# Four key tiles in one chunk for the steepest heads, weighted sums dealt in runs of 32, and an earlier turned K

## What is computed

```python
x = L0_attn_x                                    # [4, 2048, 256]
xn = _layernorm(x, axis=-1)
# attention
slopes = 2.0 ** (8.0 * arange(0, -H, -1) / H)    # H = 16: 1, 0.71, 0.5, ... 2**-7.5
scores = einsum('bhqd,bhkd->bhqk', q, k) / sqrt(16)
bias = -slopes[:, None, None] * abs(pos[None, :] - pos[:, None])
probs = softmax(scores + bias[None], axis=-1)
out = einsum('bhqk,bhkd->bhqd', probs, v)
s = out.transpose(0, 2, 1, 3).reshape(B, S, D) @ W_out.T + b_out
# experts: top 2 of 8 in one of two groups, weights normalised, plus a shared expert
y = einsum('tei,eih->teh', silu(x @ w_gate) * (x @ w_up), w_down)
g = silu(einsum('teh,te->th', y, comb) + shared)
return x + s * g
```

## Time and profile before

| | |
|---|---|
| Median of three runs (lowest, highest) | 1667.21 us (1664.34, 1673.85) |
| The profiled execution | 1676.03 us, of which the instructions span 1674.1 us |
| Busy over the span | PE 1524.8 us, ACT 1318.0 us, DVE 1010.6 us, PEld 680.6 us, POOL 496.4 us |
| Mean granted clock of TensorE | 0.976 |

### The profile page before, as it was taken

The page is one execution under the profiler, slowest core; times in us unless marked ns, Lnnn a source line. Parts: engine busy times, 40 slices in busy tenths (PEclk is TensorE's granted clock), DMA queues, the critical chain, the costliest instruction groups (busy, mean ns, idle before and its releaser), DMA issues. The chain is left out here.

```text
span 1674.1 us, 39958 instructions
## 1 busy us (share of the span) xinstructions
PE 1524.8 (91%) x15328; PEld 680.6 (41%) x15328; DVE 1010.6 (60%) x2738; ACT 1318.0 (79%) x1694; POOL 496.4 (30%) x477
## 2 busy tenths in 40 slices
PE   5898997899989999998999899989999899988996
PEld 3554564223334443343444333434443333322464
DVE  7787765988854454545445444454455444577776
ACT  5788776888888887887888788878888788788721
POOL 1222331000023343343343343434333333222053
PEclk9999998999999999999999999999999999999999
DMA  6858776233345455454444455544545554577795
GB/s 202 274 193 253 259 228 183 68 112 90 90 143 132 131 138 141 138 137 128 137 134 134 126 139 137 140 132 134 131 134 143 135 134 134 132 203 221 244 313 173
DMA packets 201089, 265.58 MB, mean 159 GB/s; under 512 B 90960, under 2 KB 158592, under 8 KB 200640
## 3 DMA queue, kind: packets, MB, share of 16 engines
q1 hardware_dynamic: 168256, 171.72, 36.8%
q0 software_dynamic: 24192, 82.86, 16.1%
q10 hardware_dynamic: 8448, 8.39, 1.4%
HBM read 180.56 MB, written 90.46 MB: 162 GB/s over the span
## 5 line engine op out<-in xcount | busy, mean ns | idle before, releaser
L1502 ACT ACTIVATE probs_att<-SC_att 128x1024 f32<-128x1024 f32 (+10 forms) x1306 | 1075.2, 911 | 181.5 <-PE SC_att L1385 160.4
L1411 PE MATMUL O_att<-probs_att,V_att 128*32 128x512 f32 (+7 forms) x8144 | 642.5, 412 | 50.3 <-DVE probs_att L1527 28.4
L1527 DVE TENSOR_TENSOR probs_att<-probs_att,decay 128x128 f32<-128x128 f32 x1024 | 264.3, 286 | 272.6 <-ACT probs_att L1502 245.9
L1411 PEld LDWEIGHTS O_att<-probs_att,V_att 128*32 128x32 f32 x8144 | 178.4, 111 | 208.7 <-issue 129.4
L1385 PE MATMUL SC_att<-Q,K_turned_att 64*128 64x512 f16 (+7 forms) x1244 | 221.6, 310 | 13.9 <-issue 5.6
L1334 POOL DMA_INDIRECT ys<-ys_att,back_of_att x144 | 144.7, 1005 | 252.9 <-ACT probs_att L1502 226.8
L1328 POOL DMA_INDIRECT x<-xn,row_of_att x144 | 142.8, 992 | 243.2 <-ACT probs_att L1502 226.3
L1385 PE MATMUL SC_att<-Q,K 64*128 64x512 f16 (+9 forms) x1154 | 201.2, 301 | 7.6 <-DVE K_turned_att L1514 7.0
L1385 PEld LDWEIGHTS SC_att<-Q,K_turned_att 64*128 64x128 f16 x1244 | 67.2, 94 | 265.2 <-ACT probs_att L1502 156.7
L1322 POOL DMA_INDIRECT x<-w_rows,owner x72 | 71.9, 999 | 333.6 <-DVE row_of_att L1576 217.3
L699 POOL TENSOR_TENSOR inverse<-qk_tok,inverse 128x512 f16<-128x512 f32 x64 | 75.6, 1189 | 171.4 <-ACT inverse L731 164.3
(11 more groups left out here) (212 smaller groups left out, 1672.4 us busy)
## 6 DMA issues: line engine op xcount, KB each, us to landing
K<-k_stack SPq DMA_DIRECT2D x86, 256.0 KB
Q<-q_stack SPq DMA_DIRECT2D x86, 256.0 KB
x<-ys POOLq DMA_DIRECT2D x32, 512.0 KB, 4.8
x<-in_x SPq DMA_DIRECT2D x24, 512.0 KB, 6.7
k_stack<-inverse SPq DMA_DIRECT2D x96, 128.0 KB
q_stack<-inverse SPq DMA_DIRECT2D x96, 128.0 KB
inverse<-k_stack SPq DMA_DIRECT2D x42, 256.0 KB
inverse<-q_stack SPq DMA_DIRECT2D x42, 256.0 KB
```

The costliest lines, as they stand in the source:

```text
L1411: mm = pe.matmul(O[VW * g:VW * (g + 1), col:col + width * len(mine)], V[par][:, k, :], spans[:, j0:j0 + BPB * (len(mine) - 1) + 1:BPB, :], ...
L1502: nc.scalar.activation(probs[home][:, side + chunk.base:side + chunk.base + chunk.width], SC[:, c % SLOTS, start:start + chunk.width], ACT ...
L1527: v.tensor_tensor(diag, diag, decay[:, head_of(chunk.head), :], ALU.mult).then_inc(faded, 1)
```

## The change

The change has five parts, all in the second stage.

1. A step takes four key tiles where two neighbouring tiles together have at most 512 queries and the next two as well (`steps_of`, `plan`). The first two tiles go to the left PSUM bank and the other two to the right one. This touches heads 0 to 2 alone: a steep head has 4 chunks of 960 or 1024 columns in place of 8 of 448 or 512 (in the first batch 4, 6 and 6 chunks in place of 8, 8 and 10). In all 1260 chunks and 794 steps are left. The columns stay the same.
2. Heads 3 to 10 are dealt to the strips in runs of 32 queries, heads 0 to 2 and 11 in runs of 64 as before (`DEALT`, `block_of`). The number of matmuls is the same, but the strips hold different counts. With 896 queries, for instance, the strips had four, four, three and three runs of 64, and have seven runs of 32 each. `store_head` follows: its pieces are 32 numbers long.
3. `fade` takes all the diagonals of a chunk in one instruction with a stride, where they lie at equal distances.
4. `turn_k` for the next head stands behind the first chunk of a head with fewer than 8 chunks. `stage_v` stays at the middle chunk.
5. `ROUTE_FROM` goes from 8 to 4 and `FF_EACH` from 11300 to 11200. The first tile of the experts is turned at column 210,240 in place of 204,160, and the last at column 1,003,776 in place of 1,005,184.

```diff
@@ -47,10 +47,10 @@
 WGU = 2 * DC * I
 WROW = WGU + D
 GROUP = 4
-ROUTE_FROM, SIDE_FROM, NORMS_AT = 8, 8, 5
+ROUTE_FROM, SIDE_FROM, NORMS_AT = 4, 8, 5
 PREFIX_TURNS, LIST_TURN, LISTED_AFTER, TILES_AFTER = (31, 36), 61, 136, 16
 FF_APART = (("turn", 2), ("gate", 3), ("down", 4))
-FF_EACH = 11300
+FF_EACH = 11200
 FF_PARTS = {"turn": ("turn", 0), "take": ("turn", 1), "gate": ("gate", 0), "up": ("gate", 0), "tanh": ("gate", 3), "hid": ("gate", 4),
             "down": ("down", 0), "y": ("down", 1)}
 MIX_FROM, MIX_TO = 364, 397
@@ -78,6 +78,7 @@
 FAR = (64, 192, 256, 256, 256, 320, 448, 576, 896, 1216, 1600, 1792)
 LIMITED = len(NEAR)
 LEFT_OUT = 2.0 ** -25
+DEALT = {h: 32 if 3 <= h < 11 else HALF for h in range(LIMITED)}
 ORDER = tuple(x for h in range(H // 2) for x in (h, H - 1 - h))
 STORED = 16 * (BPB + 1)
 
@@ -133,15 +134,17 @@
 
     if head_of(n) >= LIMITED:
         return [(kt,) for kt in range(KT)]
-    small = [window(n, kt)[1] - window(n, kt)[0] <= TB for kt in range(KT)]
+    size = [window(n, kt)[1] - window(n, kt)[0] for kt in range(KT)]
+    fits = lambda kt, count: kt + 2 * count <= KT and max(sum(size[kt:kt + count]), sum(size[kt + count:kt + 2 * count])) <= TB
     steps, kt = [], 0
     while kt < KT:
-        size = 2 if all(small[kt:kt + 2]) and len(small[kt:kt + 2]) == 2 else 1
-        steps.append(tuple(range(kt, kt + size)))
-        kt += size
+        count = 4 if fits(kt, 2) else 2 if fits(kt, 1) else 1
+        steps.append(tuple(range(kt, kt + count)))
+        kt += count
     if len(steps) % 2:
-        last = max(i for i, kts in enumerate(steps) if len(kts) == 2)
-        steps[last:last + 1] = [(kt,) for kt in steps[last]]
+        last = max(i for i, kts in enumerate(steps) if len(kts) > 1)
+        half = len(steps[last]) // 2
+        steps[last:last + 1] = [steps[last][:half], steps[last][half:]]
     return steps
 
 
@@ -204,27 +207,32 @@
         for kts in steps_of(n):
             kt = kts[0]
             if len(kts) > 1:
-                spans = [[(k, *window(n, k)) for k in kts]]
+                half = len(kts) // 2
+                spans = [[[(k, *window(n, k)) for k in side] for side in (kts[:half], kts[half:])]]
             else:
                 lo, hi = window(n, kt)
                 edges = cuts(lo, hi, kt) if limited else range(0, S + 1, TB)
-                spans = [[(kt, *edges[i:i + 2]), (kt, *edges[i + 1:i + 3])] for i in range(0, len(edges) - 1, 2)]
+                spans = [[[(kt, *edges[i:i + 2])], [(kt, *edges[i + 1:i + 3])]] for i in range(0, len(edges) - 1, 2)]
             mine, base = [], 0
-            for (ka, a0, a1), (kb, b0, b1) in spans:
-                runs = [(0, TB - (a1 - a0), ka, a0, a1), (1, 0, kb, b0, b1)]
+            for span in spans:
+                runs, first = [], base
+                for bank, side in enumerate(span):
+                    off = 0 if bank else TB - sum(q1 - q0 for _, q0, q1 in side)
+                    for k, q0, q1 in side:
+                        runs.append((bank, off, k, q0, q1))
+                        at.setdefault((n, k), base)
+                        off += q1 - q0
+                        base += q1 - q0
                 folds = [(bank, off + k * P - q0, k) for bank, off, k, q0, q1 in runs if q0 <= k * P < q1]
-                for bank, off, k, q0, q1 in runs:
-                    at.setdefault((n, k), base + (bank * (a1 - a0)))
                 mine.append(len(chunks))
-                chunks.append(Chunk(n, len(steps), runs, base, a1 - a0 + b1 - b0, folds))
-                base += a1 - a0 + b1 - b0
+                chunks.append(Chunk(n, len(steps), runs, first, base - first, folds))
             steps.append(Step(n, kts, mine))
     return chunks, steps, at
 
 
 def block_of(n):
 
-    return HALF if head_of(n) < LIMITED else TB
+    return DEALT.get(head_of(n), TB)
 
 
 def ring_slots():
@@ -1084,7 +1092,12 @@
 
     CHUNKS, STEPS, AT = plan()
     NC, NS = len(CHUNKS), len(STEPS)
-    FOLDS = [0, *itertools.accumulate(len(c.folds) for c in CHUNKS)]
+    FADES = []
+    for chunk in CHUNKS:
+        at = [AT[chunk.head, k] + k * P - window(chunk.head, k)[0] for _, _, k in chunk.folds]
+        apart = {y - x for x, y in zip(at, at[1:])}
+        FADES.append([(at[0], len(at), apart.pop())] if len(apart) == 1 else [(x, 1, P) for x in at])
+    FOLDS = [0, *itertools.accumulate(len(runs) for runs in FADES)]
     FIRST_CHUNK = [min(i for i, c in enumerate(CHUNKS) if c.head == n) for n in range(BH)] + [NC]
     LAST_STEP = [max(i for i, s in enumerate(STEPS) if s.head == n) for n in range(BH)]
     READ_AT = [None, *(STEPS[CHUNKS[FIRST_CHUNK[n]].step].chunks[-1] for n in range(1, BH))]
@@ -1374,7 +1387,8 @@
                     if c >= SLOTS:
 
                         pe.wait_ge(expd, c + 1 - SLOTS)
-                    todo = [[(off + x0 - q0, k, x0, x1, side) for x0, x1, side in pieces(head_of(n), q0, q1, k)] for _, off, k, q0, q1 in chunk.runs]
+                    todo = [[(off + x0 - q0, k, x0, x1, side) for half, off, k, q0, q1 in chunk.runs if half == bank
+                             for x0, x1, side in pieces(head_of(n), q0, q1, k)] for bank in range(2)]
                     for turn in itertools.zip_longest(*todo):
                         for bank, piece in enumerate(turn):
                             if piece is None:
@@ -1521,10 +1535,16 @@
                     chunk = CHUNKS[c]
                     dve.wait_ge(expd, c + 1)
                     home, side = PLACE[chunk.step]
-                    for _, _, k in chunk.folds:
-                        at = side + AT[chunk.head, k] + k * P - window(chunk.head, k)[0]
-                        diag = probs[home][:, at:at + P]
-                        v.tensor_tensor(diag, diag, decay[:, head_of(chunk.head), :], ALU.mult).then_inc(faded, 1)
+                    table = decay[:, head_of(chunk.head), :]
+                    for at, count, apart in FADES[c]:
+                        if count == 1:
+                            diag = probs[home][:, side + at:side + at + P]
+                            v.tensor_tensor(diag, diag, table, ALU.mult).then_inc(faded, 1)
+                        else:
+                            back = max(0, side + at + count * apart - S)
+                            rows = probs[home][:, side + at - back:side + at - back + count * apart].rearrange("p (n c) -> p n c", c=apart)
+                            diag = rows[:, :, back:back + P]
+                            v.tensor_tensor(diag, diag, table.unsqueeze(1).broadcast_to([P, count, P]), ALU.mult).then_inc(faded, 1)
 
                 def read_out(n):
                     dve.wait_ge(pv, LAST_STEP[n] + 1)
@@ -1768,10 +1788,10 @@
                             take_order()
                         if c == READ_AT[n]:
                             read_out(n - 1)
-                        if i == half and n + 1 < BH:
+                        if i == (0 if len(chunks) < 8 else half) and n + 1 < BH:
                             turn_k(n + 1)
-                            if n > 0:
-                                stage_v(n + 1)
+                        if i == half and 0 < n < BH - 1:
+                            stage_v(n + 1)
                         if b == 1 and h == NORMS_AT and i == 0:
                             norms()
                         if b > 0 and h >= SIDE_FROM and i % 2 == 0:
```

## The result

The changed kernel takes 1663.42 us (median of 20 runs, 1657.21 to 1667.62), the kernel before 1671.72 (20 runs, 1661.47 to 1680.50). The ratio is 0.994, with a 95% interval of 0.9926 to 0.9954: about 10 us off, 8 to 12, where 15.6 were forecast. The time lies in the range, 11 us above the predicted value and 0.6 us inside the forecast's own upper end. Of the 11 us, 4.5 are the base: the forecast starts from the 1667.21 us of three runs.

What follows compares the result with a forecast made beforehand. TensorE paces the experts' stretch; the first batch depends on ScalarE's next scores. 8.3 + 6.3 + 0 + 5 - 3 - 1 = 15.6 us off the 1667.2 median gives 1652 us; range 1633 to 1670, forecast's own 1640 to 1664.

Steps and rivals of the forecast that it cites:

- parts 1: Steep heads where TensorE sets the pace: fewer bursts of scores and sums save 0.92 us a head, 8.3 us.
- Part 3: Next head's turned K behind a steep head's first fade and `read_out`: counted zero, between 15 us lost and 12 gained.
- part 5: TensorE's clock around the nine steep heads: five halved stretches against three, 3 us lost, between 8 lost and 5 won.
- part 4: The first batch's three steep heads get shorter: 5 us off, bounds 0 and 9.
- part 2: Runs of 32 shorten the fullest strips of weighted sums from 485 to 1442 us: 6.3 us off.
- part 6: Pacing of the experts' work and stores in smaller pieces: together 1 us lost, between 0 and 4.
- ScalarE's view: Nine steep heads shorten from 72 to 55 us, TensorE works its backlog off in wide heads: 1639 us, chance 0.18.
- The wait for turned K: TensorE's queue behind the wide head's last sum: new waits come on top of old idle time, 1688 us, chance 0.12.
- The change does less than it says: Strips are already even enough, the bursts' saving goes into waits, first batch's 5 us left: 1662 us, chance 0.20.

Runs made afterwards that it cites:

- the experiment meant to weigh it: Changed kernel with the first batch's steep heads as before (two tiles a chunk, turned K in the middle, later routing): 1.0078 of the kernel before.

## Why the prediction was right, and where it was off

The direction, the range and most of the mechanism held; a third of the gain is missing. The table and the ratios together give, roughly, 8.0 us where parts 1, 3 and 5 said 5.3, 5.2 where part 4 said 5, about 4 where part 2 said 6.3, and 7.8 lost where part 6 said 1. That the surplus of the first covers the shortfall of part 2 is luck, as it is 11.1 us in one profile and 4.9 in the other. By the prediction's own parts:

- **Part 1, fewer bursts (8.3), and part 5, the clock (-3).** Right in kind and about right in size. The rows of the scores lost 3.5 us in the paced stretch (1.9 where overlapping ones count once; some 4 were forecast), two bursts of sums became one at about 0.2 us less, and the six heads around the steep ones are 8.0 us shorter against the 5.3 of the two terms. With runs of 64 and turned K first, the longer chunks are worth some 14 us. In the nine heads the first profile has four halved stretches and the second six; five were forecast. The mean granted clock over the timed runs is 0.980 for the kernel before beside the experiments and 0.977 after, and among the runs of one kernel 0.001 less goes with 0.6 to 1.1 us more: 2 to 3 us. The rule of the Trainium skill ("TensorE: Matmul & The Clock Gate", section "HAM oscillation — how this bites in real kernels"), taken for all nine heads, would have cost 9 us by the prediction's estimate; four and six of the nine heads showed it.
- **Part 2, runs of 32 (6.3).** This is a term that was mis-sized, and not in its columns: 6.4 to 8.7 us of the weighted sums' busy time went where 8.8 were counted. It failed where busy time was priced at its full worth because TensorE is busy 94% of the stretch. On the kernel before it bought 0.0004 of the time, 3.9 us off to 2.7 on; on the changed kernels about 4 us, not separated from the rival's nothing in either pair. The heads of the fourth line of the table, which have much of it, gained 2.2 us with everything else. The idle time took up the rest, and in which waits isn't settled. The Trainium skill ("Perfetto Trace Analysis", section "Identifying the Most-Contended Engine") says to optimize the engine with the highest occupancy first, but warns that for TensorE the busy share of matmuls is no good measure of how close it is to its limit, and takes the useful work and the busy share of weight loads instead. The case agrees with the warning: the weight loads (PEld) are busy 41% of the span, and 5 to 8 us less of matmuls were worth nothing on the kernel before. The next section ("Optimization Strategy") says to find that engine's gaps and let what they wait for start sooner, and that is what the runs bear out, with 28 us.
- **Part 3, the earlier turned K (0).** Right in sum and near in its pieces: waits of 1.52 to 1.92 us where 1.6 was worked out, second pieces of 1.01 us in head 0 and 0.4 in head 1 where 1.35 and 0.75 were, 20.5 us idle in the nine windows against 23. The place decides much more than the zero tells: 25 us are lost with turned K in the middle and 13 won with it ahead of the first fade.
- **Part 4, first batch (5).** Right: 5.2 us over the six heads, read from their lengths; the time of the experiment meant to weigh it measured something else, though the six heads in it go back to 114.2 us. Its three steep heads take 3.5, 6.2 and 6.5 us where 4.0 and twice 7.2 were worked out, 8.2 us less than before, and the wide heads behind them give 3 us back.
- **Part 6, small things (-1).** The other term that failed. Stores are no dearer (2.54 us against 2.51). The prediction found no row that splits packets by size, but the page of the profile does: 108,368 are under 512 bytes now, 90,960 were before, and the stores hold SP no longer for it. But the pacing, taken at 0.5 us, put the experts' parts at other chunks, and head 8, where they fall differently, lost 7.8 us (5.7 and 9.8 in the two profiles). The prediction counted the columns that the experts' work has beside it, and not at which chunk of which head each part falls. That line alone is more than the 5.6 us between forecast and result; how much of it is the places alone is not shown.

Of the rivals, ScalarE's view fell: the nine steep heads became 19.8 us shorter, and the three wide heads behind them got longer (the six heads together gained 8.0). The wait for turned K did not make the kernel slower, since the old waits went with it; with turned K in the middle it is 15 us slower than before, 25 slower than the changed one. "The change does less than it says" named 1662, which is nearer to the time than the forecast's 1652, but that is the base: by the gain, 10 us lie midway between its 5 and the forecast's 15.6. Its first half holds in part, since strips bring little; its second does not, since the bursts' saving is there.

## What to carry to other kernels

A busy share of 94% doesn't make each microsecond of an engine worth one: look whether the freed time sits ahead of a wait, and try it alone. Where two engines hand over at a boundary, write down what stands ahead of the awaited instruction in the other engine's queue; putting turned K, then the hidden values, ahead of copies and reciprocals that could wait was worth 28 us on top of the 10 of the change itself, a part of it as clock. And an edit that renumbers chunks moves everything that is scheduled by them: look where each part falls before and after, and compare the same head in kernels with the same plan before reading a gain into it.
